# w1 of a mixture-of-experts layer fetched per tile into two buffers, where all eight experts' w1 lay resident

## What is computed

```
x = x + tanh(g_xattn) * xattn(layernorm(x), ctx)        # additive attention over 77 context rows
# the second half, with h = layernorm(x):
probs = softmax(h @ router.T); top 2 of 8 experts per token
for eid in range(8):
    w = weight of eid for each token (0 where it was not picked)
    out += w * (gelu(h @ w1[eid].T) @ w2[eid].T)        # w1[eid]: 1024 x 256, w2[eid]: 256 x 1024
x = x + tanh(g_ffn) * out
```

## Time and profile before

| | |
|---|---|
| median of three runs | 667.19 us (666.21 to 667.31) |
| profiled execution | span 666.7 us |
| busy over the span | PE 85%, DVE 61%, ACT 55%, PEld (weight load) 44%, POOL 17% |
| DMA over the span | mean 63 GB/s; 42.02 MB moved |

### The profile page before, as it was taken

One profiled execution on the slowest core, in us unless ns is written; L12 is line 12 of the kernel. 1 busy time (PEld: TensorE's weight loads), 2 busy tenths in 40 slices (PEclk: granted clock), 3 DMA queues, 4 the chain that ended last, 5 costly groups with the idle time before them and its releaser, 6 DMA issues.

```text
span 666.7 us, 9922 instructions
## 1 busy us (share of the span) xinstructions
PE 564.8 (85%) x2850; PEld 291.3 (44%) x2851; DVE 405.9 (61%) x1176; ACT 366.9 (55%) x365; POOL 114.5 (17%) x98
## 2 busy tenths in 40 slices
PE   3777685766679988889979988699999999999993
PEld 2312121120123432333333565467777666666773
DVE  4899988988868897788887565122222333222321
ACT  0699999999997997998999312011111111111110
POOL 2000000013001160101250115111111111122111
PEclk9798999698999997899999999799999999999998
DMA  3006993002002012102030133312222221221221
GB/s 117 32 1 250 421 403 72 33 17 97 0 1 49 9 67 56 17 0 47 12 102 23 17 65 95 85 19 38 33 32 32 33 39 32 32 32 32 33 28 19
DMA packets 26426, 42.02 MB, mean 63 GB/s; under 512 B 3840, under 2 KB 23296, under 8 KB 24352
## 3 DMA queue, kind: packets, MB, share of 16 engines
q1 hardware_dynamic: 18768, 31.72, 14.2%
q0 software_dynamic: 7632, 9.98, 9.4%
HBM read 27.31 MB, written 14.38 MB: 63 GB/s over the span
## 4 chain that ended last, share of the span: by engine, by line
PE 45%; issue 14%; DVE 9%; ACT 4%; DMA 4%; POOL 3%; SPq 2%; DVEq 1%; ACTq 0%; POOLq 0%
PE y_bank L632 18%; PE h_ps L622 16%; PE rho L578 5%; PE hT_ps L643 4%; DVE hbuf L783 3%; DMA out<-y_sb,meta 2%; ACT hbuf L479 2%; POOL row_scratch L432 2%; ACT hbuf L481 1%; PE hT_ps L616 1%; DMA xs<-row_scratch 1%; DMA row_scratch<-rows,slot 1%; PE misc L598 1%; POOL out L442 1%; SPq L381 1%
## 5 line engine op out<-in xcount | busy, mean ns | idle before, releaser
L479 ACT ACTIVATE hbuf<-hbuf 128x1536 f32<-128x1536 f32 (+2 forms) x160 | 248.0, 1577 | 31.5 <-DVE hbuf L783 31.2
L783 DVE TENSOR_SCALAR hbuf<-featT,txtb 128x512 f32<-128x512 f32 (+1 forms) x519 | 214.7, 481 | 22.0 <-PE rho L578 21.2
L578 PE MATMUL rho<-hbuf,wpad 128*32 128x512 f32 x1232 | 176.5, 648 | 52.7 <-ACT hbuf L481 29.4
L498 ACT ACTIVATE hg<-h_ps 128x512 f32<-128x512 f32 x82 | 48.8, 596 | 228.6 <-PE h_ps L622 225.4
L632 PE MATMUL y_bank<-w_sb,hgT 128*128 x672 | 158.0, 387 | 2.3 <-DVE y_sb L939 1.6
L622 PE MATMUL h_ps<-w_sb,xsT 128*128 x328 | 151.0, 599 | 0.2
L632 PEld LDWEIGHTS y_bank<-w_sb,hgT 128*128 128x128 f32 x672 | 125.8, 193 | 31.0 <-issue 15.4
L442 POOL DMA_INDIRECT out<-y_sb,meta x42 | 67.7, 1612 | 382.4 <-DVE y_sb L939 309.8
L578 PEld LDWEIGHTS rho<-hbuf,wpad 128*32 128x32 f32 x1232 | 29.3, 112 | 162.9 <-ACT hbuf L481 76.9
L622 PEld LDWEIGHTS h_ps<-w_sb,xsT 128*128 128x128 f32 x328 | 58.6, 191 | 70.2 <-issue 70.2
L948 DVE COPY hgT<-hT_ps 128x512 f32<-128x512 f32 x82 | 52.8, 686 | 46.7 <-PE hT_ps L643 46.0
(11 more groups left out here) (125 smaller groups left out, 203.2 us busy)
## 6 DMA issues: line engine op xcount, KB each, us to landing
w_sb<-in_w SPq DMA_DIRECT2D x16, 1024.0 KB, 21.9
xs<-row_scratch SPq DMA_DIRECT2D x41, 132.5 KB
row_scratch<-pad SPq DMA_DIRECT2D x17, 132.5 KB, 18.4
hg<-in_x SPq DMA_DIRECT2D x4, 512.0 KB, 3.5
x_res<-in_x SPq DMA_DIRECT2D x4, 512.0 KB, 4.7
out<-x_res SPq DMA_DIRECT2D x4, 512.0 KB
out<-y_sb,meta POOLq DMA_INDIRECT x42
row_scratch<-rows,slot POOLq DMA_INDIRECT x32
```

Of the source, the lines that this page charges most:

```text
L479: ins = s.activation(h, h, ACT.Tanh)
L498: s.activation(hg[:, 512 * c:512 * (c + 1)], h_ps[:, 512 * c:512 * (c + 1)], ACT.Gelu).then_inc(hg_ok, 1)
L578: ins = t.matmul(rho[32 * j:32 * j + 32, :], wpad[:, c, 31 - r:63 - r], hbuf[:, k % HB, j, :], start=(k == 0), stop=(last and c == DC - 1) ...
L783: ins = v.tensor_scalar(hbuf[:, k % HB, j:j + 1, :], featT[:, c, bass.ds(q, 1), :], txtb[:, c, bb, CG * r + j:CG * r + j + 1], None, ALU.add)
```

## The change

`w1_sb`, which held w1 of all eight experts, is gone, and `w1_st`, with room for two, stands in its place. The eight loads of w1 at the start are gone. `xs_load` now also reads the tile's expert from `tab_e` on SP, waits until `turned_h` of tile i-2 is done (so that the buffer is free: up(i-2) has long been done then), and fetches 1 MB, that expert's w1, into buffer i mod 2. `up` waits for that fetch (`w1_in`) before its first half, reads the buffer at a fixed address, and no longer reads `tab_e`. Each of the 41 tiles fetches its own w1, also where the expert is that of a tile before.

```
-        w1_sb = sb("w1_sb", [P, E, DC, H])
+        w1_st = sb("w1_st", [P, 2, DC, H])
...
+        w1_in = [sem("w1_in0"), sem("w1_in1")]
...
             for e in range(E):
-                sp.dma_start(w1_sb[:, e], w1[:, e]).then_inc(w_in, 16)
                 sp.dma_start(w2_sb[:, e], w2[:, e]).then_inc(w_in, 16)
...
                 r = sp.value_load(tab_r[0:1, bass.ds(i, 1)], min_val=0, max_val=NROWS - P)
                 sp.dma_start(xs[:, par, :], scratch[bass.ds(r, P), :]).then_inc(xs_in[par], 16)
+                e = sp.value_load(tab_e[0:1, bass.ds(i, 1)], min_val=0, max_val=E - 1)
+                if not (isinstance(i, int) and i <= 2):
+                    sp.wait_ge(hT_ok, 2 * (i - 1))
+                sp.dma_start(w1_st[:, par], w1[:, bass.ds(e, 1)].rearrange("p o c m -> p (o c) m")).then_inc(w1_in[par], 16)
...
-            def up(i, c2, e):
-                pe.wait_ge(xsT_ok, i)
+            def up(i, par, count, c2):
+                if c2 == 0:
+                    pe.wait_ge(w1_in[par], 16 * count)
+                    pe.wait_ge(xsT_ok, i)
                 for c in range(DC):
                     ins = t.matmul(h_ps[:, 512 * c2:512 * (c2 + 1)], xsT[:, c, :],
-                                   w1_sb[:, bass.ds(e, 1), c, 512 * c2:512 * (c2 + 1)],
+                                   w1_st[:, par, c, 512 * c2:512 * (c2 + 1)],
...
-            pe.wait_ge(w_in, 16 * 2 * E)
+            pe.wait_ge(w_in, 16 * E)
```

More of the change, by code:

```diff
@@ L661, in quarter @@
                         m, step = PE_F[k]
-                        i = tile(q, m)[0]
+                        i, par, count = tile(q, m)
                         if step in ("up0", "up1"):
-                            up(i, int(step[-1]), expert(i))
+                            up(i, par, count, int(step[-1]))
                         elif step in ("down0", "down1"):
@@ L670, in step @@
             def step(this, following, mid=lambda: None, late=lambda: None):
[L671 to L674, removed]
+                i, par, count = this
+                up(i, par, count, 0)
+                up(i, par, count, 1)
                 mid()
```

## The result

| | before | after |
|---|---|---|
| median (14 runs each) | 667.25 us (663.44 to 670.53) | 670.77 us (667.57 to 673.49) |
| ratio, 95% interval | | 1.005 (1.0032 to 1.0068) |
| span of the profiled execution | 666.7 us | 669.6 us |
| PE's wait before tile 15's rows | 6.16 us | 4.34 us |
| step of the tail | 7.98 us | 7.98 us |

The change costs about 3.5 us, between 2.1 and 4.5 by the interval. The forecast was 669.3.

What follows compares the result with a forecast made beforehand. PE's work was taken to bound the tail, with SP's loads holding PE up before tile 15 and at quarter ends. 1.1 + 1.0 = 2.1 us on 666.7 gives 668.8, plus 0.5 for the median: 669.3 us; range 666.0 to 676.0.

Steps and rivals of the forecast that it cites:

- The early loads: At the start: removing eight 1 MB loads, hidden under ACT, about 2.4 us of DMA time each, gains nothing.
- Rival 4: Early part: fewer loads free DMA and SBUF, ACT's 2.2 us waits for DVE are won; 665.0 us, chance 0.10.
- PE's table reads: On PE before up: removing them gains nothing, since the tail has no PE idle time to win back.
- A lone fetch: Any 1 MB w1 fetch: estimated at 4.6 us, or 5.8 if it meets the whole of an add's data.
- The tail: Its 25 steps: the fetch is in time, the add loses about 0.5 us under 1.46 of cover; costs nothing.
- Rival 2: Tail: the fetch comes late for up, 0.3 us a step, 7.5 us in all; 675 us, chance 0.12.
- Rival 3: Tail: the add waits for all 2.4 us of a fetch's data, 24 us in all; 692 us, chance 0.08.
- The pads, first place: Before tile 15: SP's added register load and issue delay the eight pads and tile 15's rows, +1.1 us.
- The bound of 2.9: At the pads: cost of 2.9 us if the added SP instructions only lengthen the stretch of 0.7 us instructions.
- rival 1: At the pads and tile 8: both costs are absorbed, in SP's slow stretch and by timely landing; 667.2 us, chance 0.22.
- forecast sign: Before tile 15's rows: PE's wait grows from 6.16 to about 7.3 us if the prediction is right.
- Tile 8, second place: Quarter 3: tile 8's fetch meets POOL's add and lands late for up(8), between 0 and 1.0 us, taken as 1.0.

Runs made afterwards that it cites:

- q_only: The changed kernel with only tiles 1 to 9 (in the quarters) fetching their w1; 668.37 us, ratio 1.0001 to the kernel before.
- no_fetch14: The changed kernel without tile 14's fetch, that tile using what tile 12's left in the buffer; 668.91 us, ratio 1.0009 to the kernel before.
- pe_only: The kernel before with up reading a fixed address, without PE's table reads and without fetches; 664.79 us, ratio 0.9996 to the kernel before.
- after_reads: The changed kernel with PE's table reads kept, their result unused; 670.02 us, ratio 1.0091 to the kernel before.
- tiny14: The changed kernel with tile 14's fetch alone cut to 64 of 1024 columns, SP's instructions kept; 670.99 us, ratio 1.0039 to the kernel before.
- tiny_fetch: The changed kernel with all 41 fetches cut to 64 of 1024 columns, two whole loads at the start; 665.36 us, ratio 1.0013 to the kernel before.
- m_only: The changed kernel with only tiles 10 to 14 fetching, experts 0 and 1 loaded at the start; 674.11 us, ratio 1.0077 to the kernel before.
- before_again: The unchanged kernel before, profiled a second time; 667.79 us in one run.

## Why the prediction was right in sign and short in size

- **The early loads, removed at nothing.** Agrees with q_only and no_fetch14, which lack those loads and aren't faster. That the loads alone give nothing was not tried by itself. Rival 4 falls: it needed a kernel of 665.0 us.
- **PE's table reads, at nothing.** Right, by pe_only (0.9996) and after_reads.
- **A lone fetch, 4.6 us.** Right: 4.6 at the least and 4.8 in the median.
- **The tail, nothing.** Right in nearly all steps: 7.98 us, `keep_meta` later by 0.55 (0.5 was forecast), DVE's idle time down to 0.91 (about 1.0). Wrong in one step of most profiles, which took 0.4 to 1.0 us more (0.55 in the profile after): the prediction worked out the add's delay from one step and took it for all. Rival 2 falls: the fetch is issued at 513.22 and its tile starts two steps behind the up at 504.17, at 520.14, 6.9 us later, and PE never waits for it. Rival 3 falls in its price (24 us), since 25 steps would have had to lose more than 1.46 us each. Its mechanism is there, though, in the one step where the add lost 1.6 us. The rule of the Trainium skill behind it (DMA: Bandwidth & Descriptors, Queues, rings and completion order: an engine works off a whole packet of one queue before it turns to the next) is neither shown nor refuted by these times.
- **The pads, first place, +1.1 "one for one".** The right place, half of the cause, and a term that was too small. The pair is 1.2 us in the pad interval, as forecast. What the term left out are, by the traces, the bytes: the prediction counted what tile 14's fetch does to SP and not what it does to the pads and scatters that move at the same time, though it had counted just that for the add in the tail. The place cost 2.7 to 3.9 us (no_fetch14) in place of 1.1. The bound of 2.9, "if the added ones only lengthen that stretch", is near it in size, but for a reason that is wrong: the slow stretch of SP was in one execution of before and in none of the others. With it falls rival 1, which wanted the pair to be absorbed in that stretch. It also made the forecast sign "wait grown from 6.16 to about 7.3" a bad one; it was 4.34, and against the second profile's 1.9 it has grown by 2.4.
- **Tile 8, second place, +1.0.** Too high; in the profile after it is nothing. The prediction let the fetch meet the whole of an add's data and take 5.8 us. It took 5.0, and had 5.5, since the rho block ahead of up(8) ran its 3.57 us at the low clock. The place was rightly seen as tight: the margin is half a microsecond, and tile 4, which was put at nothing, waited 0.52 us in one profile (no_fetch14). q_only (1.0001, up to 1.0022) is too coarse to tell 1.0 us from 0.
- **PE's wait for a fetch.** In the profile after, the one wait of PE for `w1_in` is at tile 14, not at tile 8, and it is for the fetch of 8.0 us. Its 0.92 us cost nothing, since PE then waits 4.34 us for the rows of tile 15 anyway.
- **The range.** Its lower edge for the author's own case, 667.8, adds 1.1 us to the span of 666.7 and forgets the 0.5 up to the median; it should be 668.3. Nothing hangs on it.

The sum of 2.1 us lies at the lower edge of the measured 2.1 to 4.5. That it comes so near is partly luck, since errors stand against each other: up to 1.0 too much at tile 8, 1.6 to 2.8 too little at the pads, and the one long step of the tail.

**Open.** How fetch 14's cost splits into the pair and the bytes: tiny14 (+2.6 us over before) and tiny_fetch (+0.9) both keep the pair at this place and differ by more than their traces do, though their intervals overlap. Why m_only (1.0077, from 1.0043) and after_reads (1.0091, from 1.0058) aren't below or level with the first comparison's 1.005; their intervals overlap with it. And what of the bytes' cost is the meeting with the pads, and what with the scatters and the add behind them: these were not moved apart.

## What to carry to other kernels

What a fetch into the double buffer cost here was set by where it stands in its queue: 40 of 41 fetches of 1 MB cost under 1.5 us together, too little to tell from nothing by the times, and the one in front of a batch that the next phase waits for cost about 3 us. Go through the issuing engine's program for places where a wait on *all* of a batch follows, and keep a large load from in front of it; count its instructions, and then also the slower landing of what moves beside it. When that batch is made faster, look in the chain for what comes last then: here it was an add behind the scatters, and half of the hoped-for gain was gone. When a step's cover is read from one step, ask how far the others scatter: one late add in 27 was enough to lengthen a step. And read a stall from two executions of the kernel before: the 6.16 us on which the forecast sign rested were 1.9 in the next one.

## What was not expected of the hardware

- In one execution every instruction of SP took about 0.7 us from 410.8 to 418.7 us, an issue of L382 as well as a register load, where an issue mostly takes 0.33 to 0.36. Single instructions of SP took up to 0.88 us in other profiles, but no whole stretch of them. The eight pads took 11.17 us of SP there (its timeline is below) and 8.59 in the second profile of the same kernel.

```profile
413.03 11.17 SPq L382 DMA_DIRECT2D row_scratch<-pad  x8
```

- A 1 MB load that takes 4.8 us in the median took 8.0 beside eight pads and four scatters. The median of the eight pads (132.5 KB each) was 4.8 us beside it, where it was 2.5 in before_again; the last of them took 2.3 to 4.7 us, or 6.28.
- A scatter instruction of the same form took 0.96 to 1.36 us on POOL in five of the fourteen profiles; in the other nine some took 2.1 to 3.7 us. Both kinds are among the profiles of the kernel before. Four of the five come from one chip, on which no scatter is long in any of the four. What decides it stays open.
- PE's granted clock was 0.50 (1.2 GHz) for stretches of a few microseconds, and one of them was at about 400 us in some executions and not in others. In the profile after it was, and `down` there took 5.30 us where it takes 3.62; in before_again it took 5.18, in the first profile of before 3.62. First the window, then the timeline:

```profile
400.00:401.00 1.00, 1.00 (x4) 0.81 (x3) 0.00 (x0) 0.00 (x0) 0.00 (x0) 0.50 0.91 173
```

```profile
399.10 5.30 PE L638 MATMUL y_bank<-w_sb,hgT 128*128 x16
```

This lies ahead of the pad interval. The two profiles of before, one with it and one without, have spans of 666.0 and 666.7 us, so it doesn't explain how they differ.
